# Turning the quantised hidden row by VectorE squares and DMA instead of TensorE, with silu as one ScalarE function, in a fused attention and FP4 feed-forward kernel

## The reference, cut to what matters

```
x = layernorm(x + attn(x)); out = layernorm(x + ffn(x))      # x: 8 x 1024 x 256, f32

attn: Q = xpos(x @ W_Q); K = xpos(x @ W_K, down); V = x @ W_V
      p = softmax(Q K^T) * 0.9 ** |n - m|;  return p @ V
ffn:  fp4_linear(x, w) = quant_dequant(x) @ quant_dequant(w)^T   # blocks of 16 along the last dim
      gate, y = fp4_linear(x, w_gate), fp4_linear(x, w_up)       # 704 columns each
      h = silu(gate) * y
      return fp4_linear(h, w_down)                               # h is quantised and then contracted
```

## Time and profile before

| what | value |
|---|---|
| median of 3 runs | 987.44 us |
| the profiled execution's own time | 987.3 us |
| its span | 985.5 us |
| TensorE (matmul) busy | 960.3 us, 97% |
| VectorE busy | 862.8 us, 88% |
| GpSimd busy | 830.5 us, 84% |
| ScalarE busy | 649.6 us, 66% |
| DMA | 111.27 MB, 113 GB/s on average |

### The profile page before, as it was taken

How to read it: one execution, slowest core, us unless ns; L and a number is a source line. 1 busy time by engine, 2 the same in 40 slices (tenths; PEclk the granted TensorE clock), 3 DMA queues, 4 the chain that set the end, 5 groups by cost and what they waited for, 6 DMA issues and landing times.

```text
span 985.5 us, 20524 instructions
## 1 busy us (share of the span) xinstructions
PE 960.3 (97%) x6002; PEld 868.2 (88%) x6002; DVE 862.8 (88%) x1995; ACT 649.6 (66%) x1576; POOL 830.5 (84%) x1034
## 2 busy tenths in 40 slices
PE   8999999999999999999999999999999999999996
PEld 7788898989998899998989889898898989889986
DVE  6979888988988988888998888898898888889986
ACT  3655766676666677666676666667666666767754
POOL 5988888898888889889888888889888888887754
PEclk9999999999999999999999999999999999999999
DMA  9124235243442425314352423523334342323300
GB/s 317 44 86 128 88 97 172 91 129 93 130 144 80 137 85 176 109 55 151 104 180 82 130 91 102 172 91 113 107 102 147 106 134 81 99 98 105 115 18 28
DMA packets 116112, 111.27 MB, mean 113 GB/s; under 512 B 12576, under 2 KB 93728, under 8 KB 114080
## 3 DMA queue, kind: packets, MB, share of 16 engines
q1 hardware_dynamic: 115312, 108.91, 34.8%
q10 hardware_dynamic: 688, 1.05, 0.3%
HBM read 69.53 MB, written 40.37 MB: 112 GB/s over the span
## 4 chain that ended last, share of the span: by engine, by line
PE 68%; DVE 12%; POOL 6%; issue 4%; DMA 4%; ACT 3%; SPq 2%; DVEq 0%; POOLq 0%; ACTq 0%
PE ps_g L641 10%; PE ps_g L642 9%; PE ps_g L643 9%; PE ps_oy L641 7%; PE ps_oy L643 7%; PE ps_oy L642 7%; PE ps_s L641 4%; PE ps_s L642 4%; PE ps_s L643 4%; PE ps_t L650 3%; DMA landing<-parking 3%; POOL q_l L2508 2%; POOL h L2485 2%; PE ps_oy L650 1%; DVE turned L1876 1%
## 5 line engine op out<-in xcount | busy, mean ns | idle before, releaser
L2485 POOL TENSOR_TENSOR h<-h,hsc 128x704 f32<-128x704 f32 x126 | 168.6, 1338 | 50.4 <-DVE h L1850 36.6
L2600 POOL TENSOR_TENSOR prob<-prob,decay_t 128x512 f32<-128x512 f32 x128 | 164.8, 1297 | 1.9 <-ACT prob L1289 1.9
L641 PE MATMUL ps_oy<-v_h,pt_h 128*128 128x256 f32 x512 | 149.3, 292 | 0.5 <-DVE pt_l L1886 0.4
L641 PE MATMUL ps_g<-wgu_h,xqt_h 128*128 128x480 f32 (+1 forms) x380 | 148.7, 391 | 0.6 <-DVE h L1819 0.5
L642 PE MATMUL ps_oy<-v_l,pt_h 128*128 128x256 f32 x512 | 144.7, 283 | 0.0
L643 PE MATMUL ps_oy<-v_h,pt_l 128*128 128x256 f32 x512 | 144.6, 282 | 0.0
L643 PE MATMUL ps_g<-wgu_h,xqt_l 128*128 128x480 f32 (+1 forms) x380 | 142.4, 375 | 0.0
L642 PE MATMUL ps_g<-wgu_l,xqt_h 128*128 128x480 f32 (+1 forms) x380 | 142.1, 374 | 0.0
L641 PE MATMUL ps_s<-k_h,q_h 128*128 128x512 f32 x256 | 102.8, 402 | 0.0
L1801 DVE SCALAR_TENSOR_TENSOR th<-th,ps_g 128x240 f32<-128x240 f32 x183 | 71.6, 394 | 33.9 <-ACT th L1219 31.4
L642 PE MATMUL ps_s<-k_l,q_h 128*128 128x512 f32 x256 | 100.2, 391 | 0.0
(11 more groups left out here) (276 smaller groups left out, 3103.6 us busy)
## 6 DMA issues: line engine op xcount, KB each, us to landing
parking<-turned SPq DMA_DIRECT2D x122, 256.0 KB, 2.0
landing<-parking SPq DMA_DIRECT2D x488, 64.0 KB, 2.0
rope_t<-rope SPq DMA_DIRECT2D x15, 1024.0 KB, 5.8
xres<-x SPq DMA_DIRECT2D x64, 128.0 KB, 2.1
out<-yout SPq DMA_DIRECT2D x63, 128.0 KB, 2.0
xin<-x_t SPq DMA_DIRECT2D x14, 512.0 KB, 4.5
first_rope<-rope SPq DMA_DIRECT2D x2, 512.0 KB, 8.2
decay_t<-decay SPq DMA_DIRECT2D x1, 960.0 KB, 12.2
```

The lines of the kernel that those rows point to most:

```text
L641: pe.matmul(dst, a_h, b_h, start=(start and i == 0), stop=False)
L2485: return tt(blocks(dst), blocks(src), sc[:, which, at:at + n].unsqueeze(2).to_broadcast([P, n, QB]), ALU.mult)
L2600: tt(prob[:, keys], prob[:, keys], decay_t[:, lo:lo + CW], ALU.mult).then_inc(decayed, 1)
```

## The change

1. A new function `turns(i)` is true for tiles 0 to 58. For these, VectorE's `turn_h` transposes h in 32x32 squares (128x640 from `h`, 128x128 from `h_last`) into the same SBUF buffer `turned` that the probabilities use (its first 768 of 1024 columns); SyncE's `park_h` writes it to DRAM (384 KB), `land_h` reads it back by four DMAs into `h_landing`; ScalarE's `h_landed_high` copies the high part (128x768, from SBUF) and VectorE's `h_landed_low` makes the low part from SBUF. TensorE's `h_transposes`, ScalarE's `h_high` and VectorE's `h_low` remain for tiles 59 to 62.
2. ScalarE applies Silu directly to all tiles, into `h`; VectorE multiplies by up (`gate_times_up`). `gated` and the buffer `th` are gone.
3. `turn` of a tile's probabilities now waits until the h that lies in `turned` is parked, and `turn_h` waits until the probabilities are parked.
4. The orders of all five engines in every step are new. On TensorE `down(five)` stands behind `gate_up(three, 1)` (behind part 2 with j = 7 and in the last batch) instead of near the head, and the second half of the scores mostly follows the first. The second norm runs a step later (`six`).

```diff
+def turns(i):
+    return 0 <= i <= LAST_TURNED            # LAST_TILE - 5
...
+            def park_h(i):
+                if turns(i):
+                    sp.wait_ge(ht_done, 2 * i + 2)
+                    wait(sp, h_landed, 16 * QUADS * (i - 1))
+                    sp.dma_start(h_parking[i % 2], h_turned).then_inc(h_parked, 16)
+            def land_h(i):
+                if turns(i):
+                    sp.wait_ge(h_parked, 16 * (i + 1))
+                    wait(sp, htl_done, 2 * i)
...
+                    for c in (0, 2, 1, 3):
+                        sp.dma_start(h_landing[c * QUAD:(c + 1) * QUAD, :]...
...
                 if s // NT == NB - 1 and j > 0:
                     scores(now, 0)
-                    down(five)
+                    scores(now, 1)
                     values_product_first(two)
                     values_product_second(two)
                     x1_transposes(three)
-                    scores(now, 1)
                     projected()
                     gate_up(three, 0)
                     gate_up(three, 1)
-                    h_transposes(four, 0)
-                    h_transposes(four, 1)
                     gate_up(three, 2)
+                    down(five)
...
-            def tanh(i, r):
+            def silu(i, r):
...
+                    nc.scalar.activation(h[:, i % 2, part(r)], gate_up_at(i, r)[:, 0], ACT.Silu).then_inc(silu_done, 1)
...
+            def h_landed_high(i):
+                if turns(i):
+                    act.wait_ge(h_landed, 16 * QUADS * (i + 1))
+                    wait(act, y_done, i)
+                    nc.scalar.copy(keys_by_quad(ht_h), h_landed_at).then_inc(hth_done, 2)
...
+            def gate_times_up(i, r):
+                if live(i):
+                    wait(dve, silu_done, PARTS * i + r + 1)
+                    hv = h[:, i % 2, part(r)]
+                    tt(hv, hv, gate_up_at(i, r)[:, 1], ALU.mult).then_inc(h_done, 1)
...
+            def turn_h(i, g):
+                if turns(i):
+                    dve.wait_ge(hq_done, 2 * i + g + 1)
+                    if g == 0:
+                        for half in range(2):
+                            wait(dve, parked[half], 16 * (crossing(i + 3) if crosses(i + 3) else 0))
+                        nc.vector.transpose(h_turned_to[:, 0:FC - 1], h[:, i % 2, 0:(FC - 1) * P]).then_inc(ht_done, 1)
...
+            def h_landed_low(i):
+                if turns(i):
+                    dve.wait_ge(hth_done, 2 * i + 2)
+                    high = keys_by_quad(ht_h)
+                    tt(keys_by_quad(ht_l), h_landed_at[:, :, 0:FC - 1, :], high[:, :, 0:FC - 1, :].bitcast(F32), ALU.subtract)
...
             def turn(i, g):
...
+                    if turns(i - 4):
+                        dve.wait_ge(h_parked, 16 * (i - 3))
```

More of the change, by code:

```diff
@@ L1420, in step @@
                 if s // NT == NB - 1 and j > 0:
+                    r2_mean(six)
                     landed_copied(two)
-                    output(six)
+                    landed_high(two, 1)
+                    r2_squares(six)
+                    x_magnitude(three)
+                    if turned is not None:
+                        rotated_high(*turned)
+                    h_magnitude(four)
+                    x1_high(three)
+                    h_landed_high(five)
+                    output(six)
@@ L1423, in step @@
                     landed_high(two, 1)
                     x_magnitude(three)
-                    r2_mean(five)
+                    h_landed_high(five)
                     h_magnitude(four)
-                    r2_squares(five)
-                    x1_high(three)
-                    if turned is not None:
-                        rotated_high(*turned)
-                    r1_mean(two)
-                    r1_squares(two)
-                    tanh(three, 0)
-                    exponential(now)
@@ L2085, in step @@
                     h_reciprocals(four)
-                    second_residual(five)
+                    row_max(now)
+                    x_shift(three)
+                    landed_low(two)
+                    x_grid(three)
+                    row_inverse(two)
+                    rot_mul(*rot, 0)
+                    rot_mul(*rot, 1)
+                    xqt_low(three)
+                    turn(one, 1)
+                    first_residual(two)
+                    h_shift(four)
+                    h_landed_low(five)
@@ L2107, in step @@
                     h_max(four)
-                    turn(one, 0)
-                    x_scales(three)
-                    row_inverse(two)
                     x_reciprocals(three)
@@ L2113, in step @@
                     turn(one, 1)
-                    second_residual(five)
+                    turn(one, 0)
                     h_reciprocals(four)
+                    row_max(now)
                     landed_low(two)
@@ L2120, in step @@
                     rot_mul(*rot, 1)
+                    xqt_low(three)
                     h_shift(four)
-                    xqt_low(three)
+                    first_residual(two)
+                    h_landed_low(five)
                     h_grid(four)
-                    first_residual(two)
-                    row_max(now)
-                    gated(three, 0)
-                    silu(three, 0)
-                    h_low(four, 0)
-                    gated(three, 1)
-                    h_low(four, 1)
@@ L2205, in step @@
+                    h_landed_low(five)
                     h_shift(four)
                     h_grid(four)
-                    v_low(c_v, 1)
-                    xqt_low(three)
-                    first_residual(two)
-                    row_max(now)
-                    gated(three, 0)
-                    silu(three, 0)
-                    h_low(four, 0)
-                    gated(three, 1)
-                    h_low(four, 1)
-                    silu(three, 1)
+                    gate_times_up(three, 0)
@@ L2217, in step @@
+                    turn_h(four, 0)
+                    turn_h(four, 1)
+                    second_residual(five)
+                    gate_times_up(three, 1)
+                    gate_times_up(three, 2)
                     x_max(two)
-                    gated(three, 2)
-                    silu(three, 2)
-                elif j == 4:
-                    turn(one, 0)
+                elif j == 6:
                     h_max(four)
@@ L2673, in step @@
                     h_quantised(four, 0)
                     r1_variance(two)
+                    r1_inverse(two)
+                    h_quantised(four, 1)
+                    r1_shift(two)
+                    decay_half(now, 0)
+                    decay_half(now, 1)
+                    landed_low(one)
+                else:
+                    x_units(three)
+                    rotate(*turned, 1)
+                    h_units(four)
+                    x_quantised(three)
+                    r2_variance(six)
+                    r2_inverse(six)
+                    r2_shift(six)
+                    rotated_low(*turned)
+                    r1_variance(two)
+                    h_quantised(four, 0)
```

1304 lines of the change are left out of this document (630 added, 674 removed).

## The result

| kernel | median us | lowest to highest | runs |
|---|---|---|---|
| before | 988.16 | 986.03 to 988.91 | 4 |
| changed | 1061.83 | 1054.67 to 1064.27 | 4 |

Ratio 1.074, 95% interval 1.068 to 1.079: the change costs 74 us, where I had forecast a gain of 18. The profiled execution has a span of 1061.5 us, 76.0 more than before.

The account below looks back on a forecast made before the run. TensorE, busy 97%, was taken to bound the kernel step by step: 987.3 - 38.4 (transposes) + 7.7 + 7 + 6 (waits around x) = 969.6 us, range 951 to 1000.

Parts of the forecast that it names:

- What the new order gives back: Three places around x where TensorE would wait longer in the new orders: +7.7, +7 and +6 us.
- (a): Seven steps with j = 5: first gate product directly behind x's transposes, 1.1 us wait each, +7.7 us.
- (b): Same wait in the last batch, seven times, with ScalarE having 0.35 us to spare: +7 us, ends 0 and 21.4.
- (c): Steps with j = 1: x's transposes stand earlier and wait for x, 6 x 1.0 = +6 us, ends 0 and 12.6.
- TensorE loses the transposes, -38.4 us, all of it on the path.: Transposes of h of tiles 0 to 58 leave TensorE, 59 x 0.65 us, saving that time in full.
- The wait in `turn` for the parked h: also nothing: VectorE's turn of the probabilities: its wait ends 2 to 3 us into the step, behind other work; costed at nothing.
- The rival for late DMA: h late behind loads of rope and x by 2.7 us, two or three steps a batch: 993 us, chance 0.03.
- `h_landed_low`, from SBUF, likewise 0.82 + 0.29.: VectorE's two subtractions for the low part of h would take 0.82 and 0.29 us, as from other sources.
- ScalarE, +2.4 us a step, covered by its idle time.: Two table loads of 1.28 us a step and changed casts on ScalarE would fit into its idle time.
- My main rival, the loads on the path: Table loads delay ScalarE's full steps, 33 x 1.28 = 42 us, giving 1012 us; chance 0.19.
- VectorE, GpSimd, TensorE busy.: Signs of a right forecast over the whole kernel: busy near 850, 830 and 920 us.

Follow-up runs that it names:

- e8: The changed kernel with h of all tiles through TensorE again and silu from tanh: the old work in the new orders; 1065.58 us.
- e7: The changed kernel with h of all tiles turned by TensorE again, nothing parked, Silu and new orders kept; 1068.92 us.
- e5: The changed kernel with the edits of e3 and e4 together; 1023.05 us.
- e3: The changed kernel with SyncE's large loads moved behind the parking and landing of h in steps 0 to 2; 1043.46 us.
- e4: The changed kernel with the low part of h filled with zeros in place of the two subtractions from SBUF; 1048.67 us.
- e15: e5 with one GpSimd rotation put back ahead of x_units in step 1 of every batch; 1016.40 us.
- e9: e5 with the second half of the scores back between x's transposes and the gate product in step 5 and the last batch, row maximum moved later; 1033.44 us.
- e1: The kernel before with Silu on ScalarE for all tiles, old orders and TensorE's transposes kept; 1105.87 us.
- e18: The kernel before without VectorE's two added passes, silu left out of the result, so no table loads for all but the last three tiles; 984.43 us.
- e11: e5 with the 1 MB load of the rotation table split into four, spread over SyncE's list in steps 1 and 5; 1049.05 us.

## Why the prediction was wrong

**The account.** The 74 us by runs: the new orders +77 (e8); Silu with its loads for the tanh and VectorE's second pass +3 (e7 less e8); h off TensorE, without its two costs, -46 (e5 less e7); these two costs +39 (the queue 18 by e3, the subtractions in SBUF 13 by e4, together 39 by e5). These steps add up because each run starts where another ends; the sizes hold for this way through the changes. Of the orders' 77, 7 are a rotation that stood in the wrong place (e15). With it, the queue and the subtractions mended, 28 us above the kernel before are left, though TensorE no longer turns h; and these 28 don't rest on where e8 has its transposes. Between the transposes of x, in the traces of e15 and of the kernel before, the steps from j = 7, 0, 1 and 4 to the next take 1.4, 1.1, 1.2 and 0.9 us longer, a step of the last batch 0.6, and the one from j = 5 1.3 us less. Which moves cost this stays open: two edits that put single moves back brought nothing or lost. An undo of the orders as a whole wasn't tried; `down` at the start of the step would need h sooner than the parking and landing bring it.

**"What the new order gives back": three places, 20.7 us.** This is the step that failed by most. The waits (a) and (b) came as described: `ps_g` behind `xqt_l` 16 times, 15.5 us, where I had 14.7; so did (c), `ps_oy` behind x in the six steps with j = 1, 1.22 to 1.32 us each. But as a price for the new orders they failed: the orders alone cost 77 us by e8. The largest waits for x stood where I had none, in the steps with j = 2 (1.9 to 3.8 us each in *changed*). And (a) and (b) were no price even by themselves, since e9 took them away and lost 10 us. The sum treated a new order as the old one plus marked spots; nothing in it could have given 77.

**"TensorE loses the transposes, -38.4 us, all of it on the path."** The term itself stands: in the new orders e7 and e5 differ by 46 us. What failed is what I read beside it, that TensorE bounds the kernel step by step. I took this from its 97%, which held for the old orders, and the change replaced these. In *changed* TensorE waits 96.3 us in 96 pieces, against 20.1 in 26 (the 9.1 of the earlier trace rows are the largest part), and its busy time fell by 3 us only: the stops added to it what the transposes took away (25 us in e8, with the same work), and so did the clock, whose mean of 0.985 over 1061.5 us is 14 us of full speed more than before was missing.

**"The wait in `turn` for the parked h: also nothing"**, and late h costs nothing. The second step that failed; it is the 36.6 us row, and 18 us of the time (e3). I had seen the large loads on the queue and priced only what comes late to `down`. I did not ask who waits for the *parking*: VectorE, through the shared `turned` buffer, with the reciprocals and so x behind it. The rival for late DMA (993, chance 0.03) named the loads of rope and x rightly, but charged the landing and `down`, and was set far too low.

**"`h_landed_low`, from SBUF, likewise 0.82 + 0.29."** The third: 0.949 + 0.765, 1.71 in place of 1.11, and 13 us of the time with the little work that e4 saves besides. In the trace of *changed* the 64x128 subtraction has two kinds of length: 34 of 59 take 0.29 to 0.40 us, 25 take 1.27 to 2.37. Beside every long one GpSimd has an instruction over many columns at work (the product over h, twice the low part of q), as with the one above, which begins at 670.01 while GpSimd works from 669.26 to 671.13. Beside the short ones GpSimd is idle, or has instructions of one column, or `h_last`, and then it is `h_last` that takes 0.98 us in place of 0.40. Without the subtractions GpSimd's 128x640 product is back at 1.282 from 1.435. The Trainium skill (SBUF — State Buffer, Who interferes with whom) has this as a rule: a VectorE instruction with two inputs in SBUF contends with a GpSimd instruction that reads SBUF, and the ports they share are an exclusive lock, held by whoever comes first. The trace agrees in both directions, by the figures just given. And the code before the change paid a copy to PSUM for the same subtraction of the probabilities (`landed_copied`). Both were there to be read beforehand.

**ScalarE, +2.4 us a step, covered by its idle time.** Right, and the one part that I had feared. ScalarE is busy 797.6 us, in the 790 to 800 foreseen; the loads are the 122 foreseen (one stands in the start), each 1.283 us with nothing around it, and without 120 of them the time falls by 2.8 us only. My main rival, the loads on the path (1012, chance 0.19), is on the right side for a wrong reason. It would have been right for the old orders: e1 less e18 gives 1.00 us a load. A drain around each switch isn't in these rows.

**VectorE, GpSimd, TensorE busy.** Foreseen 850, 830, 920; measured 896, 855, 957. The first two are mostly the contention (e4, with 18 us less work on VectorE as well: 843 and 830), the third the stops and the clock.

The range, 951 to 1000, was too narrow by 62 us. It took in bounds for each term and none for the order as such.

## What to carry to other kernels

An engine at 97% bounds a kernel in the order that it has; a change that reorders all lists is costed as a new schedule, and its first question is whether the same work in the new order keeps the time. A run like e8, which does just that, comes before any sum over parts. For a new transfer, price both ends: who waits for the data, and who waits for the buffer to come free, since large loads ahead of it on the queue delay both. And a wait that one can see is not a price: ask what stands behind the work that would fill it.

## What the runs showed of the hardware

- Two operands in SBUF on VectorE beside GpSimd: 0.29 us becomes 1.27 (up to 2.37), GpSimd's own product over 640 columns 1.28 becomes 1.44 on average, and its `h_last` 0.40 becomes 0.98 where it comes second.
- A table load takes 1.283 us, by the mean of each group of them. Its price in time was 0.02 to 0.03 us in one order (a difference within the scatter of the runs) and 1.00 in another.
- TensorE's stops came with 0.35 us of added busy time each in e8, of which 0.16 is lost overlap and little is the clock. Where the stops were longer, the clock was a cost of its own: its mean is 0.998 before, 0.995 in e8, 0.985 in *changed* and 0.975 in e11, and one stop of 3.75 us was followed by 3 us at 0.54.
- The parking of h, 384 KB, takes 2.6 us from issue to landing at the median, and 6.3 us right behind a load of 1 MB (673.71 to 680.05 in the rows above).
- A load of 1 MB in four pieces among the small transfers (e11), against one (e5): between the transposes of x of the steps with j = 1 and 2, the parking of h takes 4.6 us on average in place of 2.9, that of the probabilities 3.5 in place of 4.9. I had expected the pieces to help. They also stand at other places of the list than the one load, so their size isn't shown to be the reason.
